# Where the folded reciprocals of an attention block wait to be spread: in DRAM instead of in the on-chip memory

## The chip, the cores and the metric

The kernel runs on one core of a Trainium2 chip. The metric is device time in microseconds (us): the median of the runs of the whole program. Before the change three runs took 485.31, 489.66 and 490.71 us, so the median is 489.66 us. A further execution, the profiled one, took 484.69 us; its rows are the ones read here.

## The reference, cut to what matters

The input is one image of 256 channels with 1,024 positions. Four layers follow each other; the first three are multi-head attention with 8 heads over the 1,024 positions, the fourth is a gated channel attention that the change does not touch. In each of the first three layers

```
scores = q . k            (per head, 1024 x 1024)
attn   = softmax(scores)  = exp(scores - max) / sum(exp(scores - max))
y      = attn . v
out    = W . y + residual (and a norm before or after)
```

The division by the sum is what the changed lines serve: the kernel multiplies the unnormalised `exp . v` by the reciprocal of the sum. Everything is float32.

## The kernel before

The program is written by hand, engine by engine, with semaphores; no scheduler orders it. A layer has four blocks `b = 0..3`. A block is four units of work (four heads, one half of the query positions, 512 of them), a unit is eight steps of 128 keys. Over 128 steps per layer, TensorE computes every score tile twice: once for the row maxima (L983, reduced on VectorE at L734), and once, shifted by the maximum, for the exponentials (L1010, exponentiated on ScalarE at L589 into `E`). It then forms `E . V` for four heads at once into `PV` (L1021, sixteen matmuls in one go). GpSimd (POOL) adds the exponentials in pairs into `SUMS` (L525) and issues a DMA that adds two halves of `SUMS` (L529); TensorE sums those over partitions into the denominators.

The denominators of one block are four rows of 512 numbers, each repeated over 32 partitions (in layer 0 they come out of the `PV` product itself). For blocks 0, 1 and 2 the reciprocal goes through a relay whose DMAs are all issued by the SP queue, and each of them three times per layer, nine times in all:

- `fold_sums` (L370): the four rows of 512 are folded to 128 partitions by 16 numbers, `den_in`, so that the reciprocal is short.
- `folded_reciprocals` on VectorE (L755): `rec_out`, 128 by 16.
- `reciprocal_rows` (L375): `rec_out` goes back as four rows of 512 into partitions 0, 32, 64 and 96 of `den_sb`, 8 KB.
- `spread_reciprocals` (L382): each of the four rows is copied to 32 partitions of `rec_sb`, 256 KB. Before it, SP waits for three semaphores.
- `normalise` on POOL (L500): `att = pv_sb * rec_sb`.

Block 3 takes its reciprocals straight on VectorE (`last_block`), without the relay. The product of block 2 is the last of the relay in a layer: the output projection on TensorE (L1139 in layer 0, L1145 in layers 1 and 2) waits for it by `att_ready`. The product of block 0 stands on POOL between the sums of unit 9 and of unit 10 in layers 1 and 2; that of block 1 stands after the sums of unit 13.

The same SP queue carries the two rows of the maxima of each unit into `q_stack` (`shift_rows`, L358, 2 KB each). In the queue, block 0 has two of them between L375 and L382 and four behind L382; block 1 has L382 directly behind L375 and four more L358 behind it; block 2 has nothing behind L382 until the next layer. Further waits that touch the relay: ScalarE waits for the product of a block before it overwrites `pv_sb` (L595), and for the spread before it overwrites `den_sb` (L601).

Of the kernel before, what the change touches and what calls it, by code (L numbers as in the profile page):

```python
# [5 lines left out]
F32 = mybir.dt.float32  # L6
# [5 lines left out]
P = 128  # L12
# [6 lines left out]
DP = 32  # L19
LAYERS = 3  # L20
HEAD_DIM = (16, 32, 32)
HEADS_B = 4
# [24 lines left out]
PER_ROW = HALF // DP  # L47
# [46 lines left out]
def attention_chain(nc, x, xt, w0, w1, w2, w3, pos_bias, cols, row0, row3, out):  # L94
    ctx = ExitStack()
    with ctx:
        def sb(name, shape, dt=F32):
            return ctx.enter_context(nc.sbuf_tensor(name, shape, dt))

        def sem(name):  # L100
            return ctx.enter_context(nc.semaphore(name))
# [16 lines left out]
        den_sb = sb("den_sb", [P, HALF])  # L118
# [17 lines left out]
        rec_out = sb("rec_out", [P, PER_ROW])  # L136
# [69 lines left out]
        dens_folded, recs_folded, recs_rows, recs_spread = (sem("dens_folded"), sem("recs_folded"), sem("recs_rows"),  # L206
                                                            sem("recs_spread"))
# [107 lines left out]

        QUARTER = HALF // 2

        block = ctx.enter_context(nc.Block())

        def head_row(l, h):  # L320
# [21 lines left out]
        def _(sp):  # L342
# [29 lines left out]
            def reciprocal_rows(l, b):  # L372

                sp.wait_ge(recs_folded, FOLDED * l + b + 1)
                sp.dma_start(den_sb[0:P:DP, :].rearrange("u (d n) -> u d n", n=PER_ROW), rec_out[:, :]).then_inc(recs_rows, 16)  # L375

            def spread_reciprocals(l, b):

                sp.wait_ge(recs_rows, 16 * (FOLDED * l + b + 1))
                sp.wait_ge(att_ready, FOLDED * l + b)  # L380
                sp.wait_ge(att_tail, 2 * l)
                sp.dma_start(rec_sb[:, :],  # L382
                             den_sb[0:P:DP, :].rearrange("u (o n) -> u o n", o=1)
                             .to_broadcast([HEADS_B, DP, HALF])).then_inc(recs_spread, 16)

            for l in range(LAYERS):
# [51 lines left out]
                for j in range(9, UNITS_L):  # L438
                    shift_rows(l, j)
                    if j in (9, 13):  # L440
                        reciprocal_rows(l, (j - 9) // HEADS_B)
                    if j in (10, 13):
                        spread_reciprocals(l, (j - 10) // 3)
                    if j in (12, 15):
                        fold_sums(l, j // 3 - 3)
                reciprocal_rows(l, 2)
                spread_reciprocals(l, 2)
            for n in range(4):
                sp.wait_ge(fin_act if n % 2 else fin_dve, n // 2 + 1)
# [819 lines left out]
```

## Time and profile before

| | |
|---|---|
| median of the runs | 489.66 us (485.31 to 490.71) |
| profiled execution | 484.69 us, span 483.0 us |
| TensorE (PE) busy | 455.1 us, 94% of the span |
| VectorE (DVE) busy | 362.9 us, 75% |
| ScalarE (ACT) busy | 267.4 us, 55% |
| GpSimd (POOL) busy | 214.8 us, 44% |
| queue q1 (issued by SP) | 25.41 MB, 22.0% of 16 engines' span |
| queue q0 (issued by POOL) | 16.00 MB, 18.0% of 16 engines' span |

The span is the time from the first to the last instruction. The shares are averages over four layers with different limits; what a transfer is worth is read from the place where it is waited for. Idle time of an engine that nobody waits for costs nothing.

### The profile page before, as it was taken

To read this page: it belongs to the slowest core of one execution; us is meant where nothing else is said; L and a number is where in the kernel's file an instruction comes from. 1 tells how busy PE (TensorE), PEld (TensorE's weight loads), DVE (VectorE), ACT (ScalarE), POOL (GpSimd) and SP (SyncE) were. 2 spreads that over 40 slices of the span, in tenths; PEclk is the share of its full clock that TensorE was granted. 3 is DMA by queue.
4 is the path that set the end of the run, shared out by engine and by line. 5 is a ranking of instruction groups with operands and counts; after the bars stand their busy time and mean duration, and the time that the engine had idled before them with its cause. 6 is when DMAs were issued, how large, how long until landed. Compare 5 with 4: busy or idle time off the path is not lost.

```text
span 483.0 us, 7045 instructions
## 1 busy us (share of the span) xinstructions
PE 455.1 (94%) x2228; PEld 233.9 (48%) x2228; DVE 362.9 (75%) x700; ACT 267.4 (55%) x515; POOL 214.8 (44%) x195
## 2 busy tenths in 40 slices
PE   8898999999896989999899999999999999999996
PEld 6544444444246576544444433656544444433463
DVE  7699877876578489977776756769987776748673
ACT  3228877777622327876766672124777665765032
POOL 8300031047310005889788941002799789980100
PEclk9979999999998999999999999999999999999999
DMA  5331525103210154488954441045377865452002
GB/s 154 55 59 26 155 50 134 34 4 66 47 21 0 29 126 115 90 201 178 203 115 86 92 78 24 1 97 127 82 156 153 173 116 107 76 103 47 0 2 87
DMA packets 20657, 41.88 MB, mean 87 GB/s; under 512 B 7458, under 2 KB 8746, under 8 KB 20364
## 3 DMA queue, kind: packets, MB, share of 16 engines
q1 hardware_dynamic: 15324, 25.41, 22.0%
q0 software_dynamic: 5152, 16.00, 18.0%
q8 instruction: 18, 0.29, 0.3%
q14 instruction: 19, 0.16, 0.1%
q10 hardware_dynamic: 144, 0.02, 0.0%
HBM read 5.94 MB, written 1.05 MB: 14 GB/s over the span
## 4 chain that ended last, share of the span: by engine, by line
PE 69%; SPq 11%; DVE 7%; DMA 4%; ACT 4%; POOL 3%; issue 2%; ACTq 0%; DVEq 0%; POOLq 0%
PE S L983 16%; PE PV L1021 15%; PE S L1010 15%; SPq L338 5%; SPq L331 4%; DMA k_stack<-kL 3%; PE PV L935 3%; PE S L1145 3%; ACT E L589 3%; DVE max L734 3%; POOL SUMS L525 2%; PE M L1034 2%; PE PV L961 2%; PE S L1179 2%; PE S L961 2%
## 5 line engine op out<-in xcount | busy, mean ns | idle before, releaser
L734 DVE TENSOR_REDUCE max<-S 128x1 f32<-128x512 f32 x384 | 238.8, 674 | 11.0 <-PE S L983 10.6
L589 ACT ACTIVATE E<-S 128x512 f32<-128x512 f32 x384 | 210.7, 607 | 54.2 <-PE S L1010 46.4
L525 POOL TENSOR_TENSOR SUMS<-E 128x512 f32<-128x512 f32 x120 | 158.9, 1437 | 108.5 <-ACT E L589 108.2
L983 PE MATMUL S<-k_stack,q_stack 126*128 126x512 f32 x384 | 176.8, 474 | 8.0 <-DMA k_stack<-kL 5.6
L1010 PE MATMUL S<-q_stack,k_stack 128*128 128x512 f32 x384 | 155.1, 413 | 5.5 <-ACT E L589 4.6
L983 PEld LDWEIGHTS S<-k_stack,q_stack 126*128 126x128 f32 x384 | 72.8, 191 | 78.7 <-DVE max L734 48.7
L1021 PE MATMUL PV<-E,V 128*32 128x512 f32 x768 | 91.6, 598 | 0.0
L1010 PEld LDWEIGHTS S<-q_stack,k_stack 128*128 128x128 f32 x384 | 72.3, 190 | 34.6 <-ACT E L589 20.0
L747 DVE TENSOR_TENSOR mHL<-S,mHL 4x128 fp32r<-4x128 f32 x48 | 13.3, 278 | 48.8 <-ACT mHL L578 48.8
L1021 PEld LDWEIGHTS PV<-E,V 128*32 128x32 f32 x768 | 20.7, 109 | 46.5 <-issue 27.2
L578 ACT ACTIVATE mHL<-S 4x128 fp32r<-4x128 f32 x48 | 12.6, 263 | 49.9 <-PE S L1001 49.9
L500 POOL TENSOR_TENSOR att<-pv_sb,rec_sb 128x512 f32<-128x512 f32 x9 | 12.4, 1375 | 58.7 <-DMA rec_sb<-den_sb 58.7
L529 POOL DMA_DIRECT2D SUMS<-SUMS x30 | 26.2, 875 | 9.0 <-POOL SUMS L525 9.0
L765 DVE TENSOR_TENSOR SUMS<-SUMS,E 128x512 f32<-128x512 f32 x36 | 24.9, 692 | 6.5 <-ACT E L589 3.1
L493 POOL DMA_DIRECT2D q_stack<-SUMS x6 | 2.9, 491 | 55.3 <-PE S L1010 55.3
L935 PE MATMUL PV<-ones 128*128 128x128 f32 x128 | 19.0, 313 | 2.3 <-POOL ones L458 2.3
L935 PEld LDWEIGHTS PV<-ones 128*128 128x128 f32 x128 | 18.2, 227 | 2.8 <-POOL ones L458 2.3
L1001 PEld LDWEIGHTS S<-ident,negmax 128*4 128x4 f32 x48 | 4.0, 83 | 29.3 <-issue 26.6
L1145 PE MATMUL S<-att,W 128*128 128x512 f32 x32 | 14.3, 599 | 0.0
L1001 PE MATMUL S<-ident,negmax 128*4 128x128 f32 x48 | 13.2, 275 | 0.5 <-DVE negmax L740 0.2
L765 DVE TENSOR_TENSOR SUMS<-E 128x512 f32<-128x512 f32 x6 | 6.1, 1015 | 9.1 <-ACT E L589 9.1
L779 DVE RECIPROCAL SUMS<-M 128x256 f32<-128x256 f32 x6 | 10.1, 1726 | 3.6 <-PE M L1051 3.6
(174 smaller groups left out, 336.9 us busy)
## 6 DMA issues: line engine op xcount, KB each, us to landing
SUMS<-SUMS POOLq DMA_DIRECT2D x30, 512.0 KB, 6.0
k_stack<-kH SPq DMA_DIRECT2D x28, 128.0 KB, 2.8
q_stack<-qH SPq DMA_DIRECT2D x40, 64.0 KB, 2.0
rec_sb<-den_sb SPq DMA_DIRECT2D x9, 256.0 KB
q_stack<-qH SPq DMA_DIRECT2D x16, 128.0 KB, 2.3
k_stack<-kL SPq DMA_DIRECT2D x14, 128.0 KB, 2.9
q_stack<-mHL SPq DMA_DIRECT2D x96, 2.0 KB
k_stack<-kH SPq DMA_DIRECT2D x22, 64.0 KB, 2.3
```

Source lines behind the costliest of these rows:

```text
L331: eng.dma_start(q_stack[d * blk:d * (blk + 1), slot, cs].bitcast(F32), src[p:p + d, cs].bitcast(F32)).then_inc(done, 16)
L338: eng.dma_start(k_stack[d * blk:d * (blk + 1), slot, cs].bitcast(F32), src[p:p + d, cs].bitcast(F32)).then_inc(done, 16)
L525: pool.tensor_tensor(SUMS[:, slot, :], E[:, E_PLAN[s][0], :], E[:, E_PLAN[s + 1][0], :], ALU.add).then_inc(sum_ready, 1)
L529: pool.dma_start(SUMS[:, kept:kept + 2, :], SUMS[:, added:added + 2, :], accum_op=ALU.add).then_inc(sum_dma[j % 2], 16)
L589: act.activation(E[:, slot, :], B[:, ring_of_scores(s) % B_RING, :], ACT.Exp, scale=1.0 if l == 0 else float(HEAD_DIM[l]) ** -0.5).then_in ...
L734: dve.tensor_reduce(max8[:, m % 2, 2 * t + half:2 * t + half + 1], A[:, n % A_RING, :], AX.X, ALU.max, negate=True).then_inc(a_used, 1)
L765: dve.tensor_tensor(SUMS[:, slot, :], SUMS[:, slot, :] if t > 1 else first, E[:, E_PLAN[TILES * j + t][0], :], ALU.add).then_inc(unit_sums, 1)
L935: pe.matmul(PV[:, 0:P], ones[:, :], ones[:, :], start=True, stop=True)
L983: pe.matmul(A[:, n % A_RING, :], q_stack[0:SHIFT_ROW, slot, q0:q0 + P], k_stack[0:SHIFT_ROW, slot, k0:k0 + HALF], start=True, stop=True).t ...
L1010: pe.matmul(B[:, ring_of_scores(s) % B_RING, :], k_stack[:, slot, P * t:P * (t + 1)], q_stack[:, slot, HALF * f:HALF * (f + 1)], start=Tru ...
L1021: mm = pe.matmul(PV[DP * u:DP * (u + 1), :], V[:, t, DP * h:DP * (h + 1)], E[:, E_PLAN[32 * b + 8 * u + t][0], :], start=(t == 0), stop=(t ...
L1145: mm = pe.matmul(S[:, 2 * c + half, :], W[l][:, kc, wo + P * c:wo + P * (c + 1)], att[:, kc, HALF * half:HALF * (half + 1)], start=(kc == ...
```

## The change

A buffer of 128 by 16 float32 is made in DRAM, `rec_rows`. `reciprocal_rows` writes `rec_out` there, instead of four rows of `den_sb`; `spread_reciprocals` reads its four rows of 512 from there. Semaphores, waits, the order in every queue and the number of instructions are the same; the lines behind the new one move down by two (L375 becomes L377, L382 becomes L384, L500 becomes L502).

```
+        rec_rows = nc.dram_tensor("rec_rows", (P, PER_ROW), F32, kind="Internal").ap()
...
             def reciprocal_rows(l, b):
                 sp.wait_ge(recs_folded, FOLDED * l + b + 1)
-                sp.dma_start(den_sb[0:P:DP, :].rearrange("u (d n) -> u d n", n=PER_ROW), rec_out[:, :]).then_inc(recs_rows, 16)
+                sp.dma_start(rec_rows, rec_out[:, :]).then_inc(recs_rows, 16)
...
                 sp.dma_start(rec_sb[:, :],
-                             den_sb[0:P:DP, :].rearrange("u (o n) -> u o n", o=1)
+                             rec_rows.rearrange("(u o d) n -> u o (d n)", u=HEADS_B, o=1)
                              .to_broadcast([HEADS_B, DP, HALF])).then_inc(recs_spread, 16)
```

## Rows read from the trace of the kernel before

**Rows 1.** The page: engines' busy time and share, and the chain's shares.
```profile
span 483.0 us, 7045 instructions
...
PE 455.1 (94%) x2228; PEld 233.9 (48%) x2228; DVE 362.9 (75%) x700; ACT 267.4 (55%) x515; POOL 214.8 (44%) x195
...
PE 69%; SPq 11%; DVE 7%; DMA 4%; ACT 4%; POOL 3%; issue 2%; ACTq 0%; DVEq 0%; POOLq 0%
```
**Rows 2.** Waits: engine, line, releaser: us in total, times, longest.
```profile
POOL att L500 <- DMA rec_sb<-den_sb: 58.7, 6, 18.5
ACT pv_sb L596 <- POOL att L500: 2.9, 1, 2.9
```
**Rows 3.** Timeline of SP: start, us, instructions in a row; layers 0 and 1.
```profile
110.12 0.56 SPq L382 DMA_DIRECT2D rec_sb<-den_sb  x1
113.57 7.69 SPq L358 DMA_DIRECT2D q_stack<-mHL  x4
...
131.30 0.54 SPq L382 DMA_DIRECT2D rec_sb<-den_sb  x1
...
246.00 0.57 SPq L382 DMA_DIRECT2D rec_sb<-den_sb  x1
251.03 9.18 SPq L358 DMA_DIRECT2D q_stack<-mHL  x4
...
287.67 0.56 SPq L375 DMA_DIRECT2D den_sb<-rec_out  x1
289.50 0.53 SPq L382 DMA_DIRECT2D rec_sb<-den_sb  x1
```
**Rows 4.** Timeline of POOL: start, us; in brackets idle before and its releaser.
```profile
123.44 1.56 POOL L500 TENSOR_TENSOR att<-pv_sb,rec_sb 128x512 f32<-128x512 f32 x1
138.28 1.28 POOL L500 TENSOR_TENSOR att<-pv_sb,rec_sb 128x512 f32<-128x512 f32 x1 [13.27 <-DMA rec_sb<-den_sb]
...
255.63 1.28 POOL L500 TENSOR_TENSOR att<-pv_sb,rec_sb 128x512 f32<-128x512 f32 x1 [0.72 <-DMA rec_sb<-den_sb]
256.88 3.76 POOL L525 TENSOR_TENSOR SUMS<-E 128x512 f32<-128x512 f32 x3
260.93 1.29 POOL L525 TENSOR_TENSOR SUMS<-E 128x512 f32<-128x512 f32 x1 [0.29 <-ACT E L589]
...
296.60 1.27 POOL L500 TENSOR_TENSOR att<-pv_sb,rec_sb 128x512 f32<-128x512 f32 x1 [12.87 <-DMA rec_sb<-den_sb]
...
405.97 1.28 POOL L500 TENSOR_TENSOR att<-pv_sb,rec_sb 128x512 f32<-128x512 f32 x1 [0.54 <-DMA rec_sb<-den_sb]
...
447.01 1.28 POOL L500 TENSOR_TENSOR att<-pv_sb,rec_sb 128x512 f32<-128x512 f32 x1 [12.74 <-DMA rec_sb<-den_sb]
```
**Rows 5.** Timeline of PE and its weight loads (PEld) where projections begin.
```profile
140.75 2.43 PE L1139 MATMUL S<-W,att 128*128 128x256 f32 x10
...
299.02 1.98 PE L1145 MATMUL S<-att,W 128*128 128x512 f32 x4
299.55 0.19 PEld L1145 LDWEIGHTS S<-att,W 128*128 128x128 f32 x1 [0.24 <-issue]
...
449.55 2.84 PE L1145 MATMUL S<-att,W 128*128 128x512 f32 x6
```
**Rows 6.** Stretches: engines' busy us, then granted clock, DMA share, GB/s.
```profile
91.00:95.00 4.00, 4.00 (x26) 1.77 (x25) 2.77 (x7) 2.30 (x6) 0.00 (x0) 1.00 0.24 49
54.25:54.75 0.50, 0.50 (x8) 0.00 (x0) 0.00 (x0) 0.00 (x0) 0.00 (x0) 1.00 0.91 357
```
**Rows 7.** Page, DMA issues: tiles, count, KB each, median us to landing.
```profile
W<-w_dram SPq DMA_DIRECT2D x2, 256.0 KB, 3.3
out_dram<-E SPq DMA_DIRECT2D x4, 256.0 KB, 2.5
SUMS<-row_dram SPq DMA_DIRECT2D x1, 128.0 KB, 5.9
```
**Rows 8.** Line L450, four stores of the output: least, median, most us to landing.
```profile
DMA to landing us min/median/max: 2.0/2.5/2.7
```
**Rows 9.** Tile mHL: the issues L358, least, median and longest ns.
```profile
L358 SPq DMA_DIRECT2D q_stack<-mHL x96: 572/604/2757, 27.9 to 429.9; - x96
```
**Rows 10.** Timeline of ACT in layer 2, behind the product of block 0.
```profile
409.78 0.60 ACT L589 ACTIVATE E<-S 128x512 f32<-128x512 f32 x1 [0.28 <-POOL SUMS L525]
```

More of the change, by code:

```diff
@@ L316, in attention_chain @@
         QUARTER = HALF // 2
+        rec_rows = nc.dram_tensor("rec_rows", (P, PER_ROW), F32, kind="Internal").ap()
         block = ctx.enter_context(nc.Block())
@@ L374, in reciprocal_rows @@
                 sp.wait_ge(recs_folded, FOLDED * l + b + 1)
-                sp.dma_start(den_sb[0:P:DP, :].rearrange("u (d n) -> u d n", n=PER_ROW), rec_out[:, :]).then_inc(recs_rows, 16)
+                sp.dma_start(rec_rows, rec_out[:, :]).then_inc(recs_rows, 16)
             def spread_reciprocals(l, b):
@@ L382, in spread_reciprocals @@
                 sp.dma_start(rec_sb[:, :],
-                             den_sb[0:P:DP, :].rearrange("u (o n) -> u o n", o=1)
+                             rec_rows.rearrange("(u o d) n -> u o (d n)", u=HEADS_B, o=1)
                              .to_broadcast([HEADS_B, DP, HALF])).then_inc(recs_spread, 16)
```

## The prediction

> **What bounds the kernel now.** I read the page first. TensorE is busy for 455.1 of 483.0 us and holds 69% of the chain of work that ended last; POOL has 3% of it and DMA 4% [rows 1]. The relay of the reciprocals can only matter where its end, the product L500 on POOL, holds TensorE up, directly or through ScalarE. So next come the waits. POOL waits 58.7 us for the spread, in 6 of 9 cases, and this is the largest wait that the change can touch; who waits for the product in turn is one single entry, ScalarE for 2.9 us [rows 2]. A long wait of POOL is thus no loss by itself, and I go through the nine places by timeline.
>
> *Block 2, three times.* Issue of the spread to start of the product: 131.30 to 138.28, 289.50 to 296.60, some 7.0 us each [rows 3, 4]. The product ends at 139.56, 297.87 and 448.29. TensorE comes to the projection, with no idle time written behind its rows, at 140.75 in layer 0, where the very first matmul needs block 2. In layers 1 and 2 two matmuls with block 0 go first, and the third one's weights are loaded 0.53 us later: 299.55 in layer 1, and by the same 0.53 about 450.08 in layer 2 [rows 5]. So these products are early by 1.2, 1.7 and 1.8 us. They are hidden.
>
> *Block 1.* In layer 0 the spread is issued at 110.12 and would have landed by about 117.1, and the product starts at 123.44 because POOL is busy with sums until then; no wait for the DMA stands behind the row [rows 3, 4]. The 2.9 us of ScalarE are its wait for this product, and so are POOL's order, not the relay's. In layers 1 and 2 block 1 shows no wait either (the six waits are those of block 0 and block 2).
>
> *Block 0.* In layer 0 it is the wait of 18.5 us, with no sums behind it for a long time. In layers 1 and 2 the relay is just late: POOL is idle for 0.72 and 0.54 us [rows 4]. The spread takes longer here, 246.00 to 255.63 or 9.6 us, because POOL's own adding DMAs run beside it. After the product three sums take 3.76 us and then POOL waits 0.29 us for ScalarE [rows 4]: the lateness ends there. The only trace of it in another engine is that ScalarE idles 0.28 us for a sum in layer 2 [rows 10].
>
> **The change, part by part.** The SP queue, its order and all waits stay; two transfers per block get another memory.
>
> *L375 becomes a write to DRAM, 8 KB, nine times.* Now: issued at 287.67, and the spread that waits for it is issued at 289.50, so 1.83 us [rows 3]. No row has so small a write to DRAM. The nearest are the four stores of 256 KB, 2.0 to 2.7 us [rows 8]. Bounds: 1.8 (as now) and 2.7; I take 2.1, near the least store because the data are a thirty-second of it. Cost: +0.3 us per relay, at most +0.9. In block 0 two L358 stand between it and the spread, which hides it. In block 1 of layer 0 the next entry of the queue is issued at 113.57, 2.9 us after the spread's issue ended, so SP's longer wait delays no row of maxima.
>
> The Trainium skill speaks against this step: "DMA: Bandwidth & Descriptors", the section on the anatomy of one DMA, puts most of a DMA's fixed 2 us on the confirmation of the last write and calls HBM the heaviest target. The stores above, 2.0 us at least against the 1.83 us of the on-chip copy, agree, with a small size. By its whole 2 us the sum would be the same.
>
> *L382 reads from DRAM.* While it runs alone, the 16 DMA engines are busy to 0.24 and move 49 GB/s: four engines' worth (0.24 x 16 = 3.8), 12.8 GB/s each [rows 6]. 256 KB over that is 5.3 us, and 1.7 us of its 7.0 are fixed. While a broadcast from DRAM runs (54.25 to 54.75 lies in the load of `bias3`), the share is 0.91 at 357 GB/s: 24.5 GB/s per busy engine, so nearly twice as much [rows 6]. Source memory is the difference that I see. If the spread stays on four engines its data take 262 KB / (4 x 24.5) = 2.7 us, and with 1.7 us fixed it lands in 4.4 us, 2.6 less than now. Lower end: the two loads of 256 KB from DRAM land in 3.3 us, so 3.7 less [rows 7]. Upper end: 5.9 us, the slowest such broadcast, which stood behind two larger loads, so 1.1 less [rows 7]; and, if the receiving side or the single rows that are read set the 12.8 GB/s, 7.0 as now plus whatever DRAM adds at the start. I take 4.4 us.
>
> Whether it keeps four engines: "DMA: Bandwidth & Descriptors", on why a DMA increments its semaphore by 16, says the number of engines must divide the slowest dimension of both sides. The source has 4 rows before and after. By this rule the share stays at 0.25 and the landing at 4.4 rather than 3.3 us; the 0.24 of before agrees with it. Neither value changes the sum.
>
> *Together* a relay ends 2.6 - 0.3 = 2.3 us earlier (bounds: 3.7 earlier, 0.9 later without any gain of rate). Where that goes:
> - Block 2: TensorE was not waiting. 0 us, three times; POOL idles 2.3 us less.
> - Block 1: hidden by the sums. 0 us.
> - Block 0 of layers 1 and 2: POOL starts 0.72 and 0.54 us earlier, together 1.26 us, and gives it back at its next wait for ScalarE, where 0.29 becomes 1.01. What may reach others is ScalarE's 0.28 us. I take 0.3 us, ends 0 and 1.3.
> - The rows of maxima: one L358 took 2,757 ns to issue against a median of 604 [rows 9], in the run of four at 251.03 behind a spread [rows 3]; four engines' rings are full of the spread then. That goes away. TensorE does not show a wait for them at that place, so 0 us.
> - The other engines, the order and the bytes moved on chip: no edit.
>
> Sum: 484.69 - 0.3 = 484.4 us for the profiled execution. This execution and one run (485.31) lie some 5 us below the two others (489.66 and 490.71), with nothing in the change that would favour either level; a measurement of three runs takes its median from one or the other. I keep the level of the median shown: 489.66 - 0.3 = **489.4 us**. A change of less than about 1%, 4.9 us, cannot be told from none here.
>
> **The rivals.**
>
> *A. DRAM is late, and the projection waits (slower).* Mechanism: the write must have arrived before the read begins, so two trips to DRAM replace two on chip. If a relay ends x us later than now, block 2 costs (x - 1.2) + (x - 1.7) + (x - 1.8), and block 0 of layers 1 and 2 costs up to 2(x - 0.3), since POOL has little room there; together 5x - 5.3 us. It begins to cost at x = 0.3 and passes 1% at x = 2.0, when write and read together take 1.8 + 7.0 + 2.0 = 10.8 us. The slowest rows for them make 2.7 + 5.9 = 8.6 us [rows 7, 8]. Against it, then, all rows; for it, that no row shows packets of 64 bytes written to DRAM and read back at once. At x = 3 it gives 489.7 + 9.7 = 499.4 us. Chance 7%, most of it above 1%.
>
> *B. The spread was the hidden brake (faster).* Mechanism: four DMA engines held for 5 to 9 us at a time slow the adding DMAs and the rows of maxima, and TensorE, which idles in small pieces, feels it in the sum. For it, the 2,757 ns issue and the 1.26 us of POOL. Against it, TensorE's waits name no such DMA in the middle of a layer. Worth 1.3 us by the rows (488.4), and over 1% only if several us of small waits are in truth the DMAs': 484 us. Chance 12%, with the chance that the median of the new runs falls to the lower level above by itself.
>
> *C. It does not do what it says.* The rate of 12.8 GB/s per engine is not the source's; the spread still takes 7 us and the write 0.3 more. Block 0 of layers 1 and 2 is then 0.3 us later, within its 0.29 us of room, and the time is 489.7. It cannot be told from the forecast by the time, only by the trace. Chance 15%.
>
> **The numbers.** Forecast 66%, C 15%, A 7%, B 12%. The range: its low end is the lowest run, 485.31, less the 1.3 us of B, 484.0; its high end the highest run, 490.71, plus the 1.3 us that A costs at x = 1.3, so 492.0. About 2 in 10 are left out, A's bulk and the far part of B. Faster by over 1%: 12%. Slower: 7%. Within 1%: 81%.
>
> **What would show it.** In the new profile: the spread alone at a DMA share of 0.24 and some 98 GB/s instead of 49; from its issue to the product 4.4 us instead of 7.0 in block 2; from L377 to L384 2.1 instead of 1.83 us; POOL's waits for the spread down from 58.7 to about 50 us, with 0.72 and 0.54 gone; no L358 issue of 2.7 us; TensorE's idle time and the span the same within 1 us. I am wrong if TensorE waits for POOL before L1141 or L1147 (A), if the span falls by several us with fewer small waits of TensorE (B), or if the product of block 0 moves and ScalarE's waits for sums change by more than 1 us.

## The result and the profile after

The changed kernel takes 486.03 us (median of 20 runs, 484.12 to 493.49), the kernel before, run beside it, 488.53 us (484.81 to 491.54). The ratio is 0.9949, with a 95% interval of 0.9924 to 0.9974: a small gain, clear of noise, of some 2.5 us. It lies within the 1% that was forecast as no change; the 0.3 us forecast is too little. Ratios are formed without executions that fell in a slower state of the core, here the one of 493.49 us, while medians and ranges hold all of them.

The two profiled executions differ by much less: a span of 482.4 us against 483.0. From the page of the changed kernel:

```profile
span 482.4 us, 7045 instructions
...
PE 454.9 (94%) x2228; PEld 233.9 (48%) x2228; DVE 362.4 (75%) x700; ACT 267.5 (55%) x515; POOL 216.4 (45%) x195
...
HBM read 8.30 MB, written 1.12 MB: 20 GB/s over the span
...
PE 69%; SPq 9%; DVE 8%; ACT 4%; DMA 3%; POOL 3%; issue 2%; ACTq 0%; DVEq 0%; POOLq 0%
...
SUMS<-SUMS POOLq DMA_DIRECT2D x30, 512.0 KB, 4.9
```

TensorE's 455 us and its share of the chain stand as they were [rows 1]. The reads from DRAM rose by the nine spreads. The last row is the one that matters later: the median of POOL's adding DMAs fell to 4.9 us; the page of before has 6.0.

The waits of the changed kernel, in total, times, longest:

```profile
POOL att L502 <- DMA rec_sb<-rec_rows: 47.5, 4, 16.5
ACT E L591 <- POOL SUMS L527: 4.2, 5, 1.7
ACT pv_sb L598 <- POOL att L502: 2.9, 1, 2.9
```

POOL's wait for the spread fell from 58.7 us in six waits to 47.5 in four [rows 2]; the two that went are those of block 0 in layers 1 and 2. ScalarE's wait of 2.9 us for block 1's product in layer 0 stays.

The relay of block 2 in SP's timeline of the changed kernel, and the products on POOL:

```profile
287.16 0.32 SPq L377 DMA_DIRECT2D rec_rows<-rec_out  x1
288.56 0.54 SPq L384 DMA_DIRECT2D rec_sb<-rec_rows  x1
```

```profile
254.10 1.59 POOL L502 TENSOR_TENSOR att<-pv_sb,rec_sb 128x512 f32<-128x512 f32 x1
255.35 4.04 POOL L527 TENSOR_TENSOR SUMS<-E 128x512 f32<-128x512 f32 x3
260.39 1.29 POOL L527 TENSOR_TENSOR SUMS<-E 128x512 f32<-128x512 f32 x1 [1.00 <-ACT E L591]
...
293.58 1.59 POOL L502 TENSOR_TENSOR att<-pv_sb,rec_sb 128x512 f32<-128x512 f32 x1 [10.35 <-DMA rec_sb<-rec_rows]
```

From L377 to L384 it is 1.40 us, not more than the 1.83 of the on-chip copy but less; of the 0.43 us less, 0.24 are the issue itself, 0.32 us against 0.56 [rows 3]. From the issue of the spread to the product it is 5.0 us against 7.1 [rows 3, 4]; in layers 0 and 2 it is 4.7 and 4.8. Block 0's product starts with no wait behind it, and POOL gives the time back at its next wait for ScalarE: 0.29 us became 1.00 [rows 4], as worked out.

Two stretches of block 2's spread, in layer 0 and in layer 1, alone on the engines (busy us of each engine, clock, DMA share, GB/s):

```profile
132.00:134.00 2.00, 2.00 (x15) 0.70 (x18) 1.69 (x4) 1.59 (x4) 0.00 (x0) 1.00 0.28 97
291.00:292.00 1.00, 1.00 (x11) 0.32 (x13) 0.86 (x2) 0.88 (x2) 0.00 (x0) 1.00 0.26 100
```

97 and 100 GB/s against 49, at shares of 0.28 and 0.26: still about four engines (0.28 x 16 = 4.5, 0.26 x 16 = 4.2), so 21.6 and 24 GB/s per busy engine where it had been 12.8 [rows 6]. And the longest issue of a row of the maxima (tile `mHL`) is down from 2,757 ns to 1,317 [rows 9]:

```profile
L360 SPq DMA_DIRECT2D q_stack<-mHL x96: 572/585/1317, 27.8 to 429.4; - x96
```

So most steps of the trace came out, and yet the median moved eight times as far as the forecast. One pair of profiles does not show why.

### The profile page after: what moved, and what is told of

It is laid out like the page before. It is cut to its first block, busy times and chain, and to the rows that moved or that the text cites. A ratio compares the mean times of both kernels' runs of the same rounds, so it can differ in the third digit from the quotient of the medians.

```text
span 482.4 us, 7045 instructions
## 1 busy us (share of the span) xinstructions
PE 454.9 (94%) x2228; PEld 233.9 (48%) x2228; DVE 362.4 (75%) x700; ACT 267.5 (55%) x515; POOL 216.4 (45%) x195
## 4 chain that ended last, share of the span: by engine, by line
PE 69%; SPq 9%; DVE 8%; ACT 4%; DMA 3%; POOL 3%; issue 2%; ACTq 0%; DVEq 0%; POOLq 0%
PE S L985 17%; PE PV L1023 15%; PE S L1012 15%; SPq L340 4%; SPq L333 4%; PE PV L937 3%; DMA k_stack<-kL 3%; PE S L1147 3%; ACT E L591 3%; DVE max L736 3%; PE M L1036 2%; POOL SUMS L527 2%; PE PV L963 2%; DVE SUMS L767 2%; PE S L1181 2%
## 5 line engine op out<-in xcount | busy, mean ns | idle before, releaser
L736 DVE TENSOR_REDUCE max<-S 128x1 f32<-128x512 f32 x384 | 238.9, 674 | 10.7 <-PE S L985 10.4
L502 POOL TENSOR_TENSOR att<-pv_sb,rec_sb 128x512 f32<-128x512 f32 x9 | 14.4, 1599 | 47.5 <-DMA rec_sb<-rec_rows 47.5
```

The lines of the kernel that those rows point to most:

```text
L736: dve.tensor_reduce(max8[:, m % 2, 2 * t + half:2 * t + half + 1], A[:, n % A_RING, :], AX.X, ALU.max, negate=True).then_inc(a_used, 1)
```

## The experiments

The theories. **D**, the rival B of the prediction put at one place: in layers 1 and 2 POOL issues unit 11's adding DMA (L529) within a fraction of a microsecond of block 1's spread; the four engines that carry the spread are then shared by the two, and the denominators of block 2 on TensorE (L1034) need the sum. **H**: any rows behind the spread on its four rings. **R**: block 0's relay ends earlier. **N**: nothing on the path. The first profile of before speaks for N: unit 11's DMA is issued at 268.76 and lands 9.4 us later, at 278.2, and L1034 runs at 279.12. The room is 1.0 us, with no wait. Alone, as unit 10's at 262.52, such a DMA lands after 4.5 us. POOL, SP and TensorE in that profile:

```profile
268.76 0.87 POOL L529 DMA_DIRECT2D SUMS<-SUMS  x1 [0.30 <-POOL SUMS L525]
```

```profile
268.81 0.56 SPq L382 DMA_DIRECT2D rec_sb<-den_sb  x1
```

```profile
279.12 1.92 PE L1034 MATMUL M<-SUMS,ones 128*32 128x512 f32 x16
```

**Before against itself.** No edit.

> The kernel before, unchanged, timed against itself, and a second profile of it. All theories: ratio 1.000 with an interval that holds 1, which tells how small a difference five rounds can show. Theory H (the rings' hold: the spread from on-chip memory fills the rings of four DMA engines for over 5 us, rows of the maxima that are issued behind it land late and in some executions TensorE waits for them): the spread over executions is large here, some profiles show TensorE waiting for q_stack<-mHL in the middle of layers 1 and 2, and an L358 issue of over 2 us shows again. Theory N (nothing on the path; the 0.5% is how the samples fell): no such wait.

488.32 us, ratio 0.9990 (0.9948 to 1.0031). The second profile of the same program shows what the first did not. PE, then POOL, then SP, then the landing of unit 11's adding DMA (L529, least, median and most of one):

```profile
281.80 1.92 PE L1034 MATMUL M<-SUMS,ones 128*32 128x512 f32 x16 [2.21 <-DMA SUMS<-SUMS]
```

```profile
257.07 1.27 POOL L500 TENSOR_TENSOR att<-pv_sb,rec_sb 128x512 f32<-128x512 f32 x1 [1.77 <-DMA rec_sb<-den_sb]
...
269.80 0.87 POOL L529 DMA_DIRECT2D SUMS<-SUMS  x1 [0.30 <-POOL SUMS L525]
...
281.80 2.51 POOL L525 TENSOR_TENSOR SUMS<-E 128x512 f32<-128x512 f32 x2 [2.38 <-DMA SUMS<-SUMS]
```

```profile
269.21 0.56 SPq L382 DMA_DIRECT2D rec_sb<-den_sb  x1
```

```profile
DMA to landing us min/median/max: 11.9/11.9/11.9
```

The same DMA took 11.9 us instead of 9.4, and TensorE, at its denominators, stood for 2.21 us. The room of 1.0 us in the first profile was used up and more. POOL waits for the same DMA for 2.38 us. In layer 2 of the same execution L1034 shows no such wait.

What differs is which of the two transfers was issued first. In the first profile POOL's DMA went 0.05 us ahead of the spread (268.76 and 268.81), in the second 0.59 us behind it (269.80 and 269.21), because POOL had waited 1.77 us for block 0's spread instead of 0.72 [rows 4]. In layer 2 of the second profile it went 0.07 us ahead again and landed after 9.1 us. The later profiles with block 1 on chip agree: counted with these two, there are eight places where POOL's DMA was 0.03 to 0.07 us ahead, and in all of them it landed after 8.7 to 9.9 us. No run sets this order by itself.

**The changed kernel again.** No edit.

> The changed kernel, unchanged, timed once more, and a second profile. Theory H: 0.995 again (0.992 to 0.998), no L360 issue over 2 us, no wait of TensorE for q_stack<-mHL outside the starts of the layers. Theory N: 1.000 within 0.3%. The spread alone at a DMA share near 0.13 and 50 GB/s, as in the first profile.

486.71 us, 0.9967 (0.9933 to 1.0002): by itself not clear of 1, with the first comparison a gain of 0.3 to 0.5%. Unit 11's DMA was issued at 268.20 in both profiles of the changed kernel and landed after 8.5 and 8.4 us; L1036 runs at 278.60 in the first. The room is 1.9 us instead of 1.0, and neither profile has the wait. Block 0's product in layer 1, which had no wait behind it in the first profile, waits 1.26 us here (48.6 us of POOL's waits for the spread, in five), so that wait is not always gone after the change. And this execution is 1.9 us longer than the first (span 484.3 and 482.4) with nearly the same waits: in layer 1 TensorE's granted clock fell to half, 1.2 GHz, for some 3 us, after TensorE had idled 0.48 of the 2 us before. The same stretch in the first profile was at 1.00.

```profile
288.00:290.00 2.00, 2.00 (x10) 0.61 (x13) 1.79 (x5) 1.45 (x3) 0.00 (x0) 0.53 0.08 14
```

**Held as long, relay early.** Behind the spread from DRAM, with waits of SP for `held` ahead of each `rec_rows` write and each second spread, so that the DMAs keep their order:

```
+ sp.dma_start(held_sb, rec_rows[..., 0:384] spread as above).then_inc(held, 16)
```

> The changed kernel with a second spread from DRAM right behind the first, into a buffer that nobody reads (384 of 512 columns): the relay ends as early as after the change, but the DMA engines are held nearly as long as before it. Theory H (what helped is the shorter hold of the rings): back to the time of before, ratio 0.998 to 1.003. Theory R (what helped is that the relay ends 2.6 us earlier, so POOL starts 0.7 and 0.5 us earlier): stays at 0.995. Theory N: 1.000, like the changed kernel.

485.89 us, 1.000 (0.9963 to 1.0036). Its median is 1.7 us below that of the kernel before beside it (487.55) and its ratio is 1: the twelve executions scatter from 484.32 to 490.81. It does not tell H from N, and R, which asked for 0.995, is just outside the interval. POOL waits for the spread 47.8 us in four waits, as after the change. Unit 11's DMA took 6.1 us in layer 1, where it was issued 0.37 us ahead of the spread, and 9.2 in layer 2, 0.22 us behind it; L1047 waited in neither.

**On chip, four DMAs of 32 partitions.**

```
+ for u in range(4):
+     sp.dma_start(rec_sb[32*u:32*(u+1), :], den_sb[32*u:32*u+1, :] spread over 32)
```

> The kernel before with the spread in four DMAs of 32 partitions each, still out of den_sb, so that each may use 16 engines: no DRAM at all. SP issues 3 DMAs more per spread, some 1.8 us. If the number of engines is what the four rows of the source cap, each part shows a share near 1.0 and the data of all four take about 1.3 us at 12.8 GB/s per engine. Theory H and R: the gain needs no DRAM, ratio 0.993 to 0.997. Theory N: 1.000. If on-chip source rows are limited by the row itself and not by the engines, the spread takes 5 us as before, ratio 1.000.

497.20 us, 1.0173 (1.0117 to 1.0228), a loss clear of noise, and all theories missed. Two of its waits, and the spread of block 2 alone:

```profile
PE M L1035 <- DMA SUMS<-SUMS: 6.1, 2, 3.7
PE S L1011 <- DMA q_stack<-mHL: 2.5, 3, 1.2
```

```profile
134.00:136.00 2.00, 2.00 (x18) 0.54 (x18) 1.61 (x4) 1.98 (x4) 0.00 (x0) 1.00 0.88 27
```

All engines are busy (0.88) and move 27 GB/s, 1.9 each; two us later it is 50 GB/s at 0.77. Four engines at four rows make 49 GB/s, so on chip more engines at each row brought no more bytes. What is gained in engines is lost in the hold, now of all sixteen; unit 11's DMA took 10.9 and 11.3 us in layers 1 and 2, and L1035 waited in both, 3.70 and 2.44 us. That fits the mechanism of D, but not alone: POOL had waited 4.89 us for block 0's spread in layer 1 and 2.59 in layer 2, so it issued unit 11's DMA only 7.3 and 9.0 us before TensorE wanted it, against 10.4 in the kernel before. The late relay of block 0 is a part of this loss.

**Block 1 through DRAM alone, and its complement.** In both functions the DRAM side is taken `if b == 1`, or `if b != 1`.

> Only block 1's reciprocals go through DRAM; those of blocks 0 and 2 stay on chip as before. Theory D (the gain is the adding DMA of unit 11, which POOL issues in layers 1 and 2 within half a microsecond of block 1's spread: four engines alternate between both, it lands 9.4 us later and in some executions nearly 12, and the denominators of block 2, L1034, need it 10.3 to 12 us after its issue): the whole gain, ratio 0.994 to 0.998, unit 11's adding DMA lands some 1 us earlier than before, no wait PE M L1034 for DMA SUMS<-SUMS. Theory R (block 0's relay ends earlier): 1.000. Theory N (nothing on the path): 1.000.

> The complement: blocks 0 and 2 through DRAM, block 1 on chip as before. Theory D: 1.000 (0.998 to 1.002), and in some profiles a wait of 2 us of L1034 for the adding DMA in layer 1 or 2, as before. Theory R: the whole gain, 0.995 to 0.997, and POOL's waits of 0.72 and 0.54 us gone. Theory N: 1.000 and no such waits.

Block 1 alone: 485.25 us, 0.9940 (0.9909 to 0.9971), the whole gain with a third of the edit. Unit 11's DMA took 7.3 us in layer 1, although it was issued 1.01 us behind the spread, and 8.6 in layer 2, and L1034's line has no wait for it; POOL's waits for the spread stand as before (59.7 us, six). Blocks 0 and 2: 487.00 us, 0.9979 (0.9945 to 1.0014), not told from no change; POOL's waits are at 48.9 us, near the 47.5 of the changed kernel, though block 0 still waited 1.13 us in layer 1. Unit 11's DMA took 9.9 us there, the room was 0.4. R as it was put, POOL's time given back, falls as the main cause: 10 us less of POOL's waits bring nothing that can be measured, while block 1, behind which POOL never waited, brings the gain. The two intervals overlap, so a share of blocks 0 and 2 is not excluded. And block 0 keeps a part in D. Five profiles have block 0 on chip and POOL's DMA issued 0.48 us or more behind block 1's spread in layer 1 (before against itself, four DMAs on chip, block 1 through DRAM alone, and below the collision without its bytes and the hold doubled). In all five POOL had waited 1.6 to 4.9 us for block 0's spread, and TensorE had waited 1.0 to 1.3 us for a row of the maxima near 246 to 248, while no other profile has that wait. A late block 0 opens the collision, and block 1's spread sets its price; that is read from profiles, no run was made for it.

**The collision without its bytes.** `wide = 16 if b == 1 else 512`, on chip.

> The kernel before, with block 1's spread cut to 16 of 512 columns per partition (leaves out the other columns, so block 1 is scaled by what block 0 left there), on chip: the collision without its bytes, no DRAM. Theory D: 0.994 to 0.997, unit 11's adding DMA lands in 5 to 6 us. This is the most that the collision can be worth. Theories R and N: 1.000.

485.60 us, 0.9965 (0.9927 to 1.0003). Unit 11's DMA took 5.8 us. The size fits D and the interval just holds 1. Of block 1's spread hardly anything is left to take away, so by this run the collision is worth some 0.35%, with 0 to 0.7% open, and by the run with block 1 alone 0.6%; the changed kernel, at 0.3 to 0.5%, has taken about that.

**From DRAM in four DMAs.** The edit of the on-chip one, on the changed kernel.

> The changed kernel with the spread in four DMAs of 32 partitions, each from one row in DRAM, so that each may use 16 engines. On chip the same cut made packets of 2 KB take 0.7 us and cost 1.7%. If a row of on-chip memory is the limit there and DRAM is not, a part here runs at a share near 1.0 and some 390 GB/s, all four are through within SP's issue time, and the ratio is that of the changed kernel or a little less, 0.993 to 0.998. If 16 engines reading one row are slow from DRAM too, the time is over that of before, 1.01.

488.23 us, 0.9996 (0.9961 to 1.0031). The spread is no longer slow when sixteen engines may read one row (a stretch of it ran at a share of 0.44 and 137 GB/s), and unit 11's DMA took 6.0 us, with 4 us of room. By D it should have had the gain. It does not, and I have no row for it but the three DMAs more per spread that SP issues, and one stretch of its profile: after 1.60 us of waiting for a stack copy near 241 TensorE ran from 242 to 244 at a granted clock of 0.50. Its executions as a whole were granted 0.980 on average, those of the kernel before beside it 0.981, so the clock does not explain the ratio. This is a miss of D as the whole story.

**The hold doubled in block 1.** Behind block 1's on-chip spread in layers 1 and 2 a second one of 384 columns into a spare buffer.

> The kernel before with a second on-chip spread of block 1 right behind the first in layers 1 and 2, 384 of 512 columns into a buffer that nobody reads: the relay ends when it did, the collision with unit 11's adding DMA lasts 4 us longer. Theory D: unit 11's adding DMA lands after the 10.3 us that L1034 leaves it, in every execution; L1034 waits 2 us or more per layer and unit 30 and 46 start later by as much; ratio 1.008 to 1.018. The rows of the maxima for unit 14, which had 1.2 us of room, may add to it. Theory N: 1.000.

502.11 us, 1.0298 (1.0253 to 1.0343), more than was expected. Its waits, then TensorE in layer 1, then two stretches there:

```profile
PE M L1046 <- DMA SUMS<-SUMS: 7.4, 1, 7.4
PE S L1022 <- DMA q_stack<-mHL: 7.2, 3, 5.5
```

```profile
288.00 3.40 PE L1046 MATMUL M<-SUMS,ones 128*32 128x512 f32 x16 [7.39 <-DMA SUMS<-SUMS]
```

```profile
286.00:288.00 2.00, 0.00 (x0) 0.03 (x1) 0.00 (x0) 0.00 (x0) 0.00 (x0) 0.50 0.14 32
288.00:290.00 2.00, 2.00 (x12) 0.66 (x16) 0.00 (x0) 0.00 (x0) 2.00 (x2) 0.50 0.13 26
```

In layer 1 unit 11's DMA was issued 0.89 us behind the spread, took 16.6 us, and TensorE stood 7.39 us. In layer 2 it was issued 0.07 us ahead, took 9.1 us, as ever, and instead a row of the maxima, which stands behind both spreads in SP's own queue, held TensorE for 5.5. So who loses is not the same from layer to layer; H is true as well, at this dose. This is the run that shows D's mechanism most plainly: the same place, a longer hold, and TensorE's wait grows. Part of what is over the expectation is the clock: after the wait TensorE went on at 0.50, that is 1.2 GHz, and the sixteen matmuls of L1046 took 3.40 us against 1.92; in layer 2 it stood at 0.50 from 446 to 450 as well.

**Block 1's spread 5 us later.** `if j in (10, 13)` becomes `if j in (10, 14)`, on chip.

> The kernel before with only block 1's spread moved in SP's queue behind the rows of the maxima of unit 14 (some 4 us later, when unit 11's adding DMA is all but through); no DRAM. Theory D: unit 11's adding DMA lands in 5 to 6 us, L1034 never waits, ratio 0.994 to 0.998. Block 1's product on POOL was due at 282.2; the spread lands near 281, so it holds. Theory N: 1.000. A third way: the rows of unit 15 and unit 12's adding DMA take the blow instead, 1.000.

488.50 us, 1.0030 (0.9999 to 1.0061). Against TensorE's L1034 the spread is issued 5.5 us ahead instead of 10.3. Unit 11's DMA took 4.8 us, the shortest of all, and there is no gain. The meeting moved on to unit 12's DMA, which took 10.4 us in both layers where it had taken 6.6 and 6.7, as the third way of the expectation had it, and in layer 0 block 1's product now waits for the spread, and ScalarE's wait for that product grows from 2.9 us [rows 2] to

```profile
125.77 0.60 ACT L596 ACTIVATE pv_sb<-PV 128x512 f32<-128x512 f32 x1 [3.63 <-POOL att L500]
```

0.7 us on the path (TensorE's longest wait for ScalarE in that layer grew from 1.7 to 2.4 us), which the expectation had not counted; POOL waits in all nine places. It hides a part of what D would bring, and the run decides nothing.

**The denominators one step later.** `DEN_STEPS` 111 to 112, `REC_STEPS` 117 to 118, ScalarE's copy 113 to 114.

> The kernel before with block 2's denominators one step later on TensorE (step 112 instead of 111, with ScalarE's copy and VectorE's reciprocal moved by one step too), nothing else: the collision stays, but L1034 comes some 0.7 us later and so leaves the adding DMA 11 us. Theory D: fewer and shorter waits, 0.995 to 0.999, and unit 11's adding DMA still takes 9.4 us or more. Theory N: 1.000. As block 2's relay ends 0.7 us later and had 1.7 us of room, that costs nothing.

488.81 us, 1.0018 (0.9980 to 1.0056). Unit 11's DMA took 9.3 us and had 2.2 us of room, no wait; again no gain. D's 0.999 lies inside the interval, its 0.995 does not. But 0.995 was more than this edit can give: one step is 0.7 us, and TensorE's wait in the second profile of before was 2.21, so in such an execution 1.5 us of it would remain.

**Another meeting taken away.** All profiles of before and after have TensorE waiting for a stack copy or a row of the maxima near 240 us. The changed kernel with `sp.dma_start(W12[:, :, 0:768], w2...)` moved from ahead of unit 9's rows to behind unit 15's:

> The changed kernel with one more transfer moved: the 768 KB load of the next layer's weights in layer 1, now in SP's queue behind the rows of the maxima of unit 15 instead of ahead of unit 9's. Across all profiles so far the step from unit 24 to unit 25 in layer 1, where this load meets four stack copies, POOL's adding DMA and unit 9's rows, takes 7.3 to 9.7 us, against 7.0 to 7.9 for the same step in layer 2, which has no such load. Theory W (that meeting is the larger part of the difference between executions, and has nothing to do with the reciprocals): 0.5 to 2 us more off, ratio to the kernel before 0.990 to 0.995, step of unit 25 at 7.1 to 7.5. Theory D alone: as the changed kernel, 0.995 to 0.997. If the load now delays block 2's relay, L1147 waits for POOL and it is 1.000.

484.59 us (483.41 to 487.19), 0.9924 (0.9893 to 0.9955) of before, the lowest of all versions; next to the changed kernel's 0.9949 and 0.9967 the intervals overlap, so it is likely the better one and not shown to be. Its executions were also granted more clock, 0.984 on average against 0.979 for the kernel before beside it. SP and TensorE there:

```profile
279.28 0.62 SPq L441 DMA_DIRECT2D W<-w_dram  x1
```

```profile
237.29 0.40 PE L1012 MATMUL S<-q_stack,k_stack 128*128 128x512 f32 x1
244.50 0.40 PE L1012 MATMUL S<-q_stack,k_stack 128*128 128x512 f32 x1
```

From unit 24's first score to unit 25's it is 7.21 us; in the two first profiles it was 7.73 (before) and 7.27 (after), where that step has no changed line in it. Much of the 0.6 us between those two spans is therefore this meeting, not the change. Block 0's spread, which stands behind the moved load in SP's queue, was issued at 245.47, 6.4 us ahead of the next denominators, against 5.3 in the changed kernel, and POOL did not wait for it. The projection still starts without a wait, at 298.30.

## Why the prediction was right, and where it was short

- *Block 2 is hidden, three times.* Right. The product came 2.1 us earlier after the spread's issue and TensorE did not notice: POOL's waits of 10.35 us there cost nothing.
- *Block 0 of layers 1 and 2, 0.3 us.* Right in mechanism in the first profile: the 0.72 and 0.54 us are gone and given back at once. In the second, layer 1 waits 1.26 us all the same. What the forecast could not see in one execution is that this wait reached 1.77 us in the next, and that POOL then issued unit 11's DMA behind block 1's spread. The complement run (0.9979, interval over 1) cannot tell 0.3 us from none.
- *The write to DRAM, +0.3 us.* Wrong in sign: 1.40 instead of 1.83 us, below my lower end of 1.8; for block 1 of layer 1 it is 1.53 instead of 1.81. The Trainium skill, "DMA: Bandwidth & Descriptors", the section on the anatomy of one DMA, which calls HBM the heaviest target, writes of DMAs issued from GpSimd, and these are issued by SP. This case's 8 KB write does not agree with it, and the measurement decides; but the on-chip copy also wrote four rows where the one to DRAM writes 128, and no run separates the memory from the form.
- *The read from DRAM, 4.4 us to the product.* 4.7 to 5.0 us, between 4.4 and the upper end. The rate was the forecast's: 97 and 100 GB/s (98 was written down), 21.6 and 24 GB/s per busy engine against 24.5, so the data take some 2.7 us. What was sized too small is the fixed part, 1.7 us, which is 2.0 to 2.3. The engines stayed about four, at shares of 0.26 and 0.28. The rule in the Trainium skill, "DMA: Bandwidth & Descriptors", the section on the increment of 16, had it so for a source of four rows, and the trace agrees.
- *Block 1: hidden by the sums, 0 us.* This is the step that failed: a term put at nothing. I asked who waits for the relay and found nobody, which is true. I did not ask who shares its engines at that moment and has little room. The answer was in the trace: unit 11's adding DMA is issued at 268.76, 0.05 us ahead of the spread at 268.81, and lands 1.0 us ahead of its use. Rival B named the mechanism, adding DMAs held by the spread, but its price of 1.3 us is POOL's 1.26 us of idle time at block 0, not a wait for an adding DMA; TensorE's wait for one is absent in the execution that was read and 2.2 us in the next. What the runs show for block 1 alone is 0.6% (0.3 to 0.9).
- *The rows of maxima, 0 us.* The long issue went, as forecast: 1.3 us at most in both profiles of the changed kernel, against 2.6 to 3.3 in all with block 0 on chip and the spread in one piece. That the rings were full is a reading, not shown.
- *Slower, rival A.* The relay ended earlier, not later; nothing of it was seen. Its sum is too low near its start: at x = 1.3 the terms above zero make 2.1 us, not 1.3, since the hidden products of block 2 cannot count as gains.
- *Rival C.* Excluded by 97 GB/s against 49.
- *The total.* 486.03 us lies in the range of 484.0 to 492.0 and 3.4 below the 489.4 forecast. Of that 1.1 is the level, as the three runs of before had their median 1.1 above that of twenty, and 2.2 is the gain that was missing. The range held because the executions scatter by more than either.

What stays open. A wait of 2.2 us in one of two profiles of before makes some 1 us on average, and block 0 adds at most a few tenths; the median moved by 2.5. Either the wait is more frequent than those two profiles say, or more of the small waits of the same kind go away together, or the clock has a part: two profiles of the changed kernel differ by 1.9 us through one stretch of some 3 us at half clock, and no run here takes that term out. Two kernels that should have been rid of the collision or of a part of it, the spread in four from DRAM and the denominators one step later, had no gain. For the second D promises no more than 0.7 us in some executions, which its interval allows; for the first I have no explanation. So it is shown that block 1 alone brings the gain and that a longer hold at that place costs TensorE directly; that blocks 0 and 2 bring none of it is not shown, and that the wait of L1034 accounts for all of it is argued only.

## What to carry to other kernels

A transfer that nobody waits for can still be on the path through the engines that it holds: for each one list what else is in flight, and how much room each of those has before its use, not only whether a wait is written there. Look also which of two transfers that meet is issued first, and how little would turn them round: here 0.05 us. A room of 1 us in one profile is a wait in some of the next; take a second profile of the unchanged kernel before pricing a collision at zero. When a few rows are to be copied to many partitions, look at the rate per busy engine first: sixteen engines at one on-chip row each time were slower than four at four rows.

## What the runs showed of the hardware that was not expected

- A few on-chip rows are a narrow source: 12.8 GB/s per busy engine with four engines at four rows [rows 6], and 27 to 50 GB/s in all when sixteen could take part, at shares of 0.88 and 0.77. The same rows read from DRAM gave 21.6 to 24 GB/s per busy engine with four, and 137 GB/s in a stretch where sixteen could take part.
- 8 KB of 64-byte pieces written to DRAM and confirmed took 1.40 us from issue to the next issue, the on-chip copy of the same bytes into four rows 1.83; the issue alone 0.32 against 0.56 us.
- The same 512 KB adding DMA, beside the same spread, in the same program, landed after 9.4 us in one execution and 11.9 in the next, and after 16.6 and 9.1 in two layers of one execution with the hold doubled. The short times go with an issue 0.05 and 0.07 us ahead of the spread, the long ones with 0.59 and 0.89 us behind it; alone it takes 4.5.
- TensorE's granted clock fell to 0.50 (1.2 GHz) during a wait of 7.39 us, and after one of 1.60, but stayed at 1.00 through one of 2.21 us; in the second profile of the changed kernel it fell near 288 after 0.48 us of idling.
